# Decoder layer on one core: slots as 8-byte pairs in a prefilled list, rows gathered three tiles ahead, routing in one block with the experts

## The chip, the cores and the metric

One of the cores of a Trainium2 chip runs the whole program. TensorE (PE) multiplies, VectorE (DVE), ScalarE (ACT) and GpSimd (POOL) work element by element, SyncE (SP) issues most of the DMAs, POOL those with computed addresses. The engines run their own instruction streams and meet at semaphores. The metric is the device time in microseconds of one execution; lower is better.

## The reference

The input x is 8 sequences of 512 tokens of 256 numbers (4096 tokens), with a context of 8 x 1601 rows. Everything is float32. Three layers follow each other, each `x = layernorm(x + layer(x))`:

- a mixing layer: projections, cosine and sine phases, running sums over the sequence, gates, a layernorm and a projection;
- cross attention: 16 heads of 16 over the 1601 context rows;
- a mixture of experts: a router takes the 2 best of 8 experts for each token, softmax over the two logits gives their weights, and the result is the sum over both of `w * (relu(x @ W1[e] + b1[e]) @ W2[e] + b2[e])`, with W1 256 x 1024 and W2 1024 x 256.

## The kernel before

The program has four blocks; between two of them all engines wait for each other and for the DMAs that the block waits for.

*Mixing* (lines 220 to 1025). One sequence ("batch", b = 0 to 7) a step, the next one's projections beside this one's end. ACT writes x1 (line 769), the layer's normalized result; PE turns it for the queries (`turn`, line 492), POOL stores it to DRAM as x1_all (line 399) and prepares xbo, the residual plus bias, of the next batch (line 404); q, k and v go to DRAM as well. VectorE's products and sums are at lines 911 and 916, its wait for ACT's mean_sq ahead of line 942.

*Attention* (lines 1028 to 1353). 32 rounds, one for each batch and group of four heads. SP stores a round's result and loads the heads of the round after the next (`two_rounds`, lines 1106 to 1127; the loads at 186 to 192), then one expert's W1 a batch. For each tile of 128 context rows PE makes scores (1194), VectorE their maximum (1257), ACT the exponentials and sums (1349), POOL scales v (1321), PE multiplies (1162).

*Routing* (lines 1362 to 1716), one batch a step, two batches in the pipeline. SP loads attention's output and x1 (1442, 1444) and an expert's W2 (1450). PE projects (1516), POOL adds the output bias to x1 (1469), VectorE adds both (1594), takes mean and variance (1597, 1601), ACT the root (1564, 1566), VectorE writes x2 (1625). PE turns x2 (1529), ACT copies it (1561), PE makes the logits (1537). VectorE takes the two best (1611, 1615), their one-hot masks (1638, 1644), and with PE's ranks (1545, 1547) the slot of each token in its expert's region (1658 to 1678). Each row to be computed is written to the DRAM tensor xs as 258 numbers: the 256 of x2, the token's number and its weight. ACT makes two copies of x2 in rows_out (1575), POOL fills in the numbers (1482), waits for slot_u and issues eight indirect DMAs of 128 rows (1490); it also stores x2 as the start of the sums (1479). At the end POOL fills each region's tail with pad rows (1499, 1501), while VectorE plans the 71 tiles: the first row in xs and the expert of each (1699 to 1716).

*Experts* (lines 1719 to 1963), 71 tiles of 128 rows. SP reads a tile's row number and loads its rows (`load`, 1774 and 1775). PE turns them (1805), VectorE takes number and weight out (1904, 1905), copies the turned rows (1906) and, when the tile before has left the second halves, the expert's weights (1893 to 1895) and its scaled b2 (1898). PE multiplies by W1 (1818), ACT applies relu (1845), PE multiplies by W2 (1828), VectorE scales and adds b2 (`y_out`, 1924), and POOL adds the 128 rows to sums_all with an indirect DMA (1879), one at a time. In its order VectorE runs, in the step of tile n, `take_rows` and `weights` of tile n+1 and then y_out of tile n:

```python
                        if more:
                            v.wait_ge(mm1_done, HC // 4 * n + OPEN)
                            v.wait_ge(xs_t_ready, n + 2)
                            take_rows(after)
                            v.wait_ge(mm2_done, n + OPEN)
                            v.wait_ge(xst_copied, n + 3)
                            weights(bass.ds(n + 1, 1), after)
                        v.wait_ge(y_added[h], 16 * loads_of(it, d - 2, h))
                        v.wait_ge(mm2_done, n + 1 + OPEN)
```

Then the sums are read back, normalized (1853 to 1862) and written out, within the same block. A wait on a semaphore holds all that stands behind it on its engine.

## Time and profile before

| | us |
|---|---|
| median of 3 runs (2293.61 to 2300.70) | 2298.87 |
| the profiled execution | 2301.51 |
| its span | 2299.7 |
| busy in it: PE, DVE, ACT, POOL | 2005.8, 1765.3, 1550.1, 707.9 |

The span runs from the first to the last instruction of the profiled execution; outside it lie 1.8 us. The busy time of an engine is its instructions' alone, without waits. A tenth of the span is about 230 us; the stages have other shares than the whole, so a mean over the span says little of any of them.

### The profile page before, as it was taken

To read this page: it belongs to the slowest core of one execution; us is meant where nothing else is said; L and a number is where in the kernel's file an instruction comes from. 1 tells how busy PE (TensorE), PEld (TensorE's weight loads), DVE (VectorE), ACT (ScalarE), POOL (GpSimd) and SP (SyncE) were. 2 spreads that over 40 slices of the span, in tenths; PEclk is the share of its full clock that TensorE was granted. 3 is DMA by queue.
4 is the path that set the end of the run, shared out by engine and by line. 5 is a ranking of instruction groups with operands and counts; after the bars stand their busy time and mean duration, and the time that the engine had idled before them with its cause. 6 is when DMAs were issued, how large, how long until landed. Compare 5 with 4: busy or idle time off the path is not lost. (4 is left out here: it accounts for less than half of the span.)

```text
span 2299.7 us, 43580 instructions
## 1 busy us (share of the span) xinstructions
PE 2005.8 (87%) x10638; PEld 1059.2 (46%) x10638; DVE 1765.3 (77%) x3666; ACT 1550.1 (67%) x4346; POOL 707.9 (31%) x919
## 2 busy tenths in 40 slices
PE   6988988499999999999999998886645999999993
PEld 2454555133222232222332221113535999999993
DVE  4968875399999999999999999995653555555554
ACT  3455555399999999999999999994211333333334
POOL 0001100044444444444444441111772222333331
PEclk9989989699999999999999999997767999999997
DMA  4111103746676675775766755635732222222224
GB/s 149 42 41 69 55 23 128 148 76 104 129 130 110 131 102 124 120 122 128 112 118 115 135 105 68 97 47 177 241 123 59 37 37 37 37 37 37 37 37 156
DMA packets 130113, 217.32 MB, mean 94 GB/s; under 512 B 20290, under 2 KB 100802, under 8 KB 129938
## 3 DMA queue, kind: packets, MB, share of 16 engines
q1 hardware_dynamic: 103072, 152.25, 35.7%
q0 software_dynamic: 25440, 63.46, 10.0%
q10 hardware_dynamic: 1554, 1.05, 0.2%
q8 instruction: 20, 0.33, 0.1%
q14 instruction: 27, 0.22, 0.0%
HBM read 137.97 MB, written 78.72 MB: 94 GB/s over the span
## 5 line engine op out<-in xcount | busy, mean ns | idle before, releaser
L1349 ACT ACTIVATE probs<-psum,neg_max 128x512 f32<-128x512 f32 (+1 forms) x1664 | 1112.3, 742 | 45.9 <-DVE neg_max L1257 44.7
L1257 DVE TENSOR_REDUCE neg_max<-psum 128x1 f32<-128x512 f32 (+1 forms) x1664 | 1025.4, 676 | 18.7 <-PE psum L1194 15.3
L1194 PE MATMUL psum<-qst,kst 96*128 96x512 bf16 (+1 forms) x1664 | 530.7, 391 | 100.3 <-ACT probs L1349 61.5
L1162 PE MATMUL psum<-probs,v_scaled 128*32 128x512 f32 (+1 forms) x3328 | 450.1, 614 | 9.2 <-DVE attn L1271 9.2
L1194 PEld LDWEIGHTS psum<-qst,kst 96*128 96x128 bf16 (+1 forms) x1664 | 130.3, 98 | 688.7 <-ACT probs L1349 641.2
L1349 ACT ACTIVATION_READ_ACCUMULATOR probs<-psum,neg_max 128x1 f32 (+1 forms) x1664 | 436.1, 262 | 0.0
L1845 ACT ACTIVATE hid<-psum,b 128x128 f32<-128x128 f32 x568 | 162.5, 369 | 393.2 <-PE psum L1818 392.6
L1321 POOL TENSOR_TENSOR v_scaled<-vst,inv 128x64 f32<-128x64 f32 (+1 forms) x416 | 121.6, 292 | 687.8 <-DVE inv L1225 687.8
L1879 POOL DMA_INDIRECT sums_all<-y_out,dest x71 | 154.4, 2175 | 381.2 <-DVE y_out L1924 375.4
L1818 PE MATMUL psum<-xst,w 128*128 128x128 f32 x2272 | 266.6, 276 | 0.0
L1818 PEld LDWEIGHTS psum<-xst,w 128*128 128x128 f32 x2272 | 260.8, 193 | 0.1
L1828 PE MATMUL psum<-w,hid 128*128 128x256 f32 x1136 | 256.9, 379 | 0.0
L1828 PEld LDWEIGHTS psum<-w,hid 128*128 128x128 f32 x1136 | 210.4, 190 | 25.7
L1924 DVE SCALAR_TENSOR_TENSOR y_out<-psum,weight,b_scaled 128x256 f32<-128x256 f32 x71 | 34.3, 484 | 184.4 <-issue 177.9
L1162 PEld LDWEIGHTS psum<-probs,v_scaled 128*32 128x32 f32 (+1 forms) x3328 | 66.6, 108 | 134.1 <-issue 83.2
L1894 DVE COPY w<-w_all 128x2048 f32 x71 | 98.8, 1391 | 0.0
L1182 PE MATMUL psum<-ct,xwk 128*128 128x448 f32 x208 | 96.2, 543 | 0.0
L1177 PE MATMUL psum<-xwv,ct 128*128 128x256 f32 x364 | 93.7, 379 | 0.0
L1895 DVE COPY w<-w_all 128x2048 f32 x71 | 86.2, 1215 | 0.0
L1893 DVE COPY b<-b_cols 128x8 f32 x71 | 31.7, 447 | 60.7 <-DVE xst L1906 59.6
L1177 PEld LDWEIGHTS psum<-xwv,ct 128*128 128x128 f32 x364 | 69.2, 190 | 17.7
L1288 POOL TENSOR_SCALAR k_out<-k_f 128x448 bf16<-128x448 f32 x52 | 68.9, 1326 | 19.8 <-DVE k_f L1244 19.8
(222 smaller groups left out, 2105.8 us busy)
## 6 DMA issues: line engine op xcount, KB each, us to landing
kst<-k_parts SPq DMA_DIRECT2D x384, 112.0 KB, 6.5
k_parts<-k_out POOLq DMA_DIRECT2D x52, 336.0 KB, 3.1
w_all<-in_W SPq DMA_DIRECT2D x16, 1024.0 KB
ct<-in_ctxT SPq DMA_DIRECT2D x16, 896.0 KB, 4.7
vst<-v_all SPq DMA_DIRECT2D x64, 224.0 KB, 9.1
qst<-q_parts SPq DMA_DIRECT2D x192, 64.0 KB, 5.9
v_all<-v_out POOLq DMA_DIRECT2D x13, 896.0 KB, 4.3
rows_in<-xs SPq DMA_DIRECT2D x71, 129.0 KB, 2.0
```

The costliest lines, as they stand in the source:

```text
L1162: last = pe.matmul(psum[j * PAD:(j + 1) * PAD, 6, :], v_scaled[0:r, pb, j, :], probs[0:r, pb, j, :], start=t == 0, stop=t == ST - 1)
L1177: last = pe.matmul(psum[:, 7, (t % 2) * D:(t % 2 + 1) * D], ct1[:, k, t * P:(t + 1) * P], xwv[:, k, :], start=k == 0, stop=k == C - 1)
L1182: last = pe.matmul(psum[:, 7, 0:KC], xwk[:, part, co * P:(co + 1) * P], ct1[:, part, s0:s0 + KC], start=part == 0, stop=part == 1)
L1194: pe.matmul(psum[0:r, 2 * sbuf + i, :], kst[:, h, j, t * P:t * P + r], qst[:, h, j, :], start=True, stop=True).then_inc(scores_ready, 1)
L1257: v.tensor_reduce(neg_max[0:r, sbuf, i:i + 1], psum[0:r, 2 * sbuf + i], AX_X, ALU.min) \
L1321: pool.tensor_tensor(v_scaled[0:r, pb, :, 0:DH], vst[0:r, h, t, :].rearrange("p (j d) -> p j d", j=GH), inv[0:r, pb].rearrange("p (j o) -> ...
L1349: act.activation(probs[0:r, pb, j, :], psum[0:r, 2 * sbuf + i, :], ACT.Exp, bias=neg_max[0:r, sbuf, i:i + 1], scale=-1.0, accum_out=sums[0 ...
L1818: last = pe.matmul(psum[:, 2 + 2 * h + c // 4, (c % 4) * P:(c % 4 + 1) * P], w1[:, h, k, c * P:(c + 1) * P], xst[:, h, k, :], start=k == 0 ...
L1828: last = pe.matmul(psum[:, 6 + h, 0:D], hid[:, h, c, :], w2[:, h, c, :], start=c == 0, stop=c == HC - 1)
L1845: act.activation(hid[:, h, c], psum[:, 2 + 2 * h + c // 4, (c % 4) * P:(c % 4 + 1) * P], ACT.Relu, bias=b1[:, h, c:c + 1]).then_inc(h_read ...
L1879: pool.indirect_dma_start(sums_all, bass.IndirectOffsetOnAxis(dest[:, d, :], 0), y_out[:, h], None, compute_op=ALU.add).then_inc(y_added[h ...
L1894: v.tensor_copy(w1[:, half], w1_all[:, at].rearrange("p o c h -> p (o c) h")).then_inc(w1_ready, 1)
```

## The change

- The rows tensor xs is replaced by a list: for each slot a pair (token number, weight), 8 bytes. The list is filled beforehand, in the attention block, with pairs that name pad rows with weight 0 (`no_pairs`), so that no pads are written at the end. x2 is stored in DRAM twice, as x2_rows (which ends in 128 zero rows) and as the start of the sums, both by SP. ACT's two copies and POOL's copy of the numbers fall away; the scatters write pairs.
- A tile's rows are gathered by POOL with an indirect DMA from x2_rows. SP loads the tile's part of the list three tiles ahead into one of four places, VectorE casts the numbers (`name_rows`), POOL gathers (`gather`).
- Routing and experts are one block. The routing steps stand in straight line, three batches deep: norm of batch c, choice for c-1, ranks and slots for c-2. Projection alternates between two pairs of PSUM banks and is cut in two halves around the logits. ACT writes x2 in place of VectorE. POOL waits for nothing but slots.
- The output bias of attention is added to x1 in the mixing stage by POOL, before x1 is stored, after PE has turned it.
- w2_all is allocated from the start and lends its space to the mixing and attention stages; W2 of one expert and the routing inputs of batches 0 and 1 and xWo are loaded in the attention block, the other W2 in routing steps 3 to 7. W2 comes in an order that gives each partition 8 KB in one run.
- The semaphore wo_g_ready goes; derived_ready is waited for in its place.

The diff, cut to its core (of the removed lines only some are shown; the helpers that are not shown keep their operations):

```diff
-    ROW = D + 2
-    AT_DEST, AT_WEIGHT = D, D + 1
-    xs = nc.dram_tensor("xs", [E * REGION + P, ROW], F32, kind="Internal").ap()
+    list_all = nc.dram_tensor("list_all", [E * REGION + P, 2], F32, kind="Internal").ap()
+    x2_rows = nc.dram_tensor("x2_rows", [TOKENS + P, D], F32, kind="Internal").ap()
...
-                            wait_alone(pool, (x1_ready, e + 1))
+                            wait_alone(pool, (x1t_ready, e + 1))
+                            pool.tensor_tensor(x1, x1, rows[:, XBO:XBO + 1, :].to_broadcast([P, TT, D]), ALU.add) \
+                                .then_inc(x1bo_ready, 1)
+                            wait_alone(pool, (x1bo_ready, e + 1))
...
+                    sp.dma_start(list_all, a["no_pairs"]).then_inc(list_cleared, 16)
+                    sp.dma_start(x2_rows[TOKENS:TOKENS + P], a["no_rows"]).then_inc(list_cleared, 16)
+                    for e in range(W2_EARLY):
+                        load_w2(sp, e)
...
+                        if b == B - 2:
+                            for h in range(2):
+                                sp.wait_ge(attn_stored[h], 16 * GH * 2 * (B - 1) + OPEN)
+                                load_route(sp, h)
+                            sp.dma_start(xwo, a["xWo"].rearrange("(c p) d -> p c d", p=P)).then_inc(xwo_loaded, 16)
...
+                    def route_step(c):
+                        h = c % 2
+                        if c < B and c + 2 < B:
+                            sp.wait_ge(y2_ready, c + 1)
+                            load_route(sp, c + 2)
+                        if c < B:
+                            sp.wait_ge(x2_ready, c + 1)
+                            for rows_to in (sums_all, x2_rows):
+                                sp.dma_start(rows_to[c * L:(c + 1) * L].rearrange("(p t) d -> p t d", t=TT),
+                                             x2[:, h]).then_inc(x2_stored[h], 16)
+                        for e in W2_IN_STEP.get(c, ()):
+                            load_w2(sp, e)
...
+                    def load_list(j, d):
                         row = sp.value_load(tile_row[0:1, j], min_val=0, max_val=NO_TILE)
-                        sp.dma_start(rows_in[:, h], xs[bass.ds(row, P)]).then_inc(rows_loaded[h], 16)
-                    def tile_step(n, it, d, more):
-                        h = d % 2
-                        if more:
-                            sp.wait_ge(xst_copied, n + 1)
-                            load(bass.ds(n + 1, 1), 1 - h)
-                    load(slice(0, 1), 0)
+                        sp.dma_start(list_in[:, d], list_all[bass.ds(row, P)]).then_inc(list_loaded[d], 16)
+                    def tile_step(n, it, d, left):
+                        if left >= 3:
+                            sp.wait_ge(y_scaled, n + 1 + OPEN)
+                            load_list(bass.ds(n + 3, 1), (d + 3) % DESTS)
...
+                    sp.wait_ge(plan, ROWS_PLANNED)
+                    sp.wait_ge(scattered, 16 * 2 * TT * B)
+                    for j in range(3):
+                        load_list(slice(j, j + 1), j)
...
+                    def scatter(e):
+                        pool.wait_ge(slots_ready, e + 1)
+                        for i in range(2):
+                            for t in range(TT):
+                                at = i * TT + t
+                                pool.indirect_dma_start(
+                                    list_all, bass.IndirectOffsetOnAxis(slot_u[:, e, at:at + 1], 0),
+                                    pairs[:, e, i, t, :], None).then_inc(scattered, 16)
+                    def gather(count, d):
+                        wait_alone(pool, (dest_ready, count))
+                        pool.indirect_dma_start(rows_in[:, d % 2], None, x2_rows,
+                                                bass.IndirectOffsetOnAxis(dest[:, d, :], 0)) \
+                            .then_inc(rows_loaded[d % 2], 16)
+                    def tile_step(n, it, d, left):
+                        h = d % 2
+                        if left >= 3:
+                            wait_alone(pool, (xs_t_ready, n + 2))
+                            gather(n + 4, (d + 3) % DESTS)
+                        wait_alone(pool, (y_scaled, n + 2 + OPEN), (y_added[1 - h], 16 * loads_of(it, d - 1, 1 - h)))
+                        pool.indirect_dma_start(sums_all, bass.IndirectOffsetOnAxis(dest[:, d, :], 0), y_out[:, h], None,
+                                                compute_op=ALU.add).then_inc(y_added[h], 16)
+                    for i in range(2):
+                        pool.tensor_copy(pairs[:, :, i, :, 0], dest_ids[:].rearrange("p (b t) -> p b t", b=B)) \
+                            .then_inc(numbered, 1)
+                    pool.wait_ge(numbered, 2)
+                    pool.wait_ge(list_cleared, 32)
+                    for e in range(B):
+                        scatter(e)
+                    for h in range(2):
+                        pool.wait_ge(x2_stored[h], 16 * B)
+                    for n in range(2):
+                        gather(n + 1, n)
+                    wait_alone(pool, (xs_t_ready, 1))
+                    gather(3, 2)
...
+                    def route_step(c):
+                        if 0 <= c - 2 < B:
+                            ranks(c - 2)
+                        if 0 <= c - 1 < B:
+                            turn(c - 1)
+                        if c + 1 < B:
+                            project(c + 1, (0, 1))
+                        if 0 <= c - 1 < B:
+                            route(c - 1)
+                        if c + 1 < B:
+                            project(c + 1, (2, 3))
...
+                    def route_step(c):
+                        h = c % 2
+                        if 0 <= c - 1 < B:
+                            wait(act, logits_z_ready, c - 1)
+                            act.wait_ge(x2t_ready, c)
+                            act.activation(x2t[:], psum[:, 4:6], ACT.Copy).then_inc(x2t_copied, 1)
+                        if c < B:
+                            act.wait_ge(moments2_ready, c + 1)
+                            act.activation(rstd2_ln[:], moments2[:, :, 1], ACT.Ln, bias=eps_col[:]).then_inc(act_ln2, 1)
+                            act.wait_ge(act_ln2, c + 1)
+                            act.activation(rstd2[:], rstd2_ln[:], ACT.Exp, scale=-0.5).then_inc(rstd2_ready, 1)
+                            wait(act, x2_stored[h], 32 * (c // 2))
+                            wait(act, x2t_ready, c - 1)
+                            act.wait_ge(rstd2_ready, c + 1)
+                            act.wait_ge(shift2_ready, c + 1)
+                            for t in range(TT):
+                                last = act.activation(x2[:, h, t], y2[:, t], ACT.Identity, bias=shift2[:, t:t + 1],
+                                                      scale=rstd2[:, t:t + 1])
+                            last.then_inc(x2_ready, 1)
+                        if 0 <= c - 1 < B:
+                            act.wait_ge(gap_ready, c)
+                            act.activation(egap[:], gap[:], ACT.Exp).then_inc(egap_ready, 1)
...
+                    def route_step(c):
+                        if c < B:
+                            norm_rows(c)
+                        if 0 <= c - 2 < B:
+                            slots(c - 2)
+                        if c < B:
+                            shift_rows(c)
+                        if 0 <= c - 1 < B:
+                            choose(c - 1)
...
+                    def name_rows(d, count):
+                        v.wait_ge(list_loaded[d], count)
+                        v.tensor_copy(dest[:, d], list_in[:, d, 0:1]).then_inc(dest_ready, 1)
...
+                            v.wait_ge(y_scaled, n + 1 + OPEN)
+                            scale_bias(copy_weights(bass.ds(n + 1, 1), 1 - h), (d + 1) % DESTS)
+                        if left >= 3:
+                            v.wait_ge(y_added[1 - h], 16 * loads_of(it, d - 1, 1 - h))
+                            name_rows((d + 3) % DESTS, 16 * (it + (d + 3) // DESTS + 1))
...
+        "W2": w[f + "W2"].reshape(E, -1, P, D).transpose(0, 2, 1, 3).reshape(E, P, -1),
+        "no_rows": np.zeros((P, D), np.float32),
+        "no_pairs": np.stack([slot % P + B * L, 0 * slot], axis=1).astype(np.float32),
```

## Rows read from the trace of the kernel before

**Rows 1.** The stages: length, busy us of each engine, granted clock, DMA share, GB/s.

```profile
0.00:443.20 443.20, 355.67 (x1172) 199.27 (x1172) 286.11 (x392) 218.51 (x352) 42.63 (x62) 0.91 0.28 83
443.20:1580.60 1137.40, 1052.28 (x5564) 305.94 (x5564) 1110.83 (x2256) 1118.24 (x3328) 414.95 (x689) 0.98 0.61 106
1580.60:1749.40 168.80, 82.12 (x356) 71.31 (x357) 82.07 (x385) 30.49 (x49) 95.89 (x97) 0.65 0.57 198
1749.40:2265.20 515.80, 515.70 (x3548) 482.68 (x3546) 271.40 (x562) 163.74 (x569) 152.86 (x70) 1.00 0.22 35
2265.20:2299.70 34.50, 0.00 (x0) 0.00 (x0) 14.94 (x73) 19.08 (x48) 1.55 (x1) 0.54 0.65 247
```

**Rows 2.** The chain that ended last, its tail: start us, length us, what.

```profile
2266.43 3.66 DMA sums_all<-y_out,dest
...
2277.98 2.06 ACT w_all L1862 x4
```

**Rows 3.** Groups of the routing stage: busy us, mean ns, idle before, releaser.

```profile
L1490 POOL DMA_INDIRECT xs<-rows_out,slot_u x64 | 62.7, 980 | 38.2 <-DVE slot_u L1678 20.4 <-issue 17.8
L1516 PE MATMUL psum<-xwo,at_in 128*128 128x256 f32 x128 | 42.3, 502 | 12.6 <-DMA x_in<-x_all 11.2 <-DVE y L1594 1.4
...
L1537 PE MATMUL psum<-router_w,x2t 128*128 128x8 f32 x128 | 26.5, 345 | 29.3 <-ACT x2t L1561 29.3
```

**Rows 4.** Waits of the whole run: who for whom, us, times, longest.

```profile
DVE var_c L942 <- ACT mean_sq L744: 66.4, 8, 12.7
...
ACT rows_out L1575 <- DMA xs<-rows_out,slot_u: 38.7, 6, 8.7
```

**Rows 5.** Timeline of the routing stage's opening: start, length, engine, line, operation.

```profile
1587.62 5.78 PE L1516 MATMUL psum<-xwo,at_in 128*128 128x256 f32 x16 [11.21 <-DMA x_in<-x_all]
...
1597.34 1.38 DVE L1625 TENSOR_SCALAR x<-y,moments,rstd 128x256 f32<-128x256 f32 x4 [0.67 <-ACT rstd L1566]
...
1612.67 0.17 DVE L1678 CAST slot_u<-slot_f 128x8 uint32<-128x8 f32 x1
...
1613.78 1.06 POOL L1490 DMA_INDIRECT xs<-rows_out,slot_u  x1 [10.28 <-DVE slot_u L1678]
```

**Rows 6.** Timeline of the routing stage's end.

```profile
1720.56 0.97 POOL L1490 DMA_INDIRECT xs<-rows_out,slot_u  x1 [0.30 <-issue]
...
1742.37 0.35 SPq L1775 DMA_DIRECT2D rows_in<-xs  x1
...
1744.21 15.98 SPq L1775 DMA_DIRECT2D rows_in<-xs  x4
...
1749.45 5.09 PE L1818 MATMUL psum<-xst,w 128*128 128x128 f32 x32
```

**Rows 7.** Issue to landing of the loads of one tile's rows.

```profile
DMA to landing us min/median/max: 1.9/2.0/4.7
```

**Rows 8.** Timeline of one steady expert tile.

```profile
2004.51 0.49 DVE L1924 SCALAR_TENSOR_TENSOR y_out<-psum,weight,b_scaled 128x256 f32<-128x256 f32 x1 [2.52 <-issue]
...
2005.75 2.18 POOL L1879 DMA_INDIRECT sums_all<-y_out,dest  x1 [5.07 <-DVE y_out L1924]
...
2008.90 0.34 DVE L1898 TENSOR_SCALAR b_scaled<-b_all,weight 128x256 f32 x1
```

**Rows 9.** Issue to landing of the summing DMA, 2000 to 2100 us.

```profile
DMA to landing us min/median/max: 4.2/4.4/4.5
```

**Rows 10.** Timeline of the mixing stage: three products beside a POOL operation.

```profile
216.73 5.77 DVE L916 TENSOR_TENSOR w_all<-w_all 128x1024 f32<-128x1024 f32 x3
...
222.53 1.23 DVE L916 TENSOR_TENSOR w_all<-w_all,key_cos 128x1024 f32<-128x1024 f32 x1
```

**Rows 11.** The DMA queues: packets, MB, share of 16 engines.

```profile
q1 hardware_dynamic: 103072, 152.25, 35.7%
...
q10 hardware_dynamic: 1554, 1.05, 0.2%
```

**Rows 12.** The DMA queue's timeline early in the attention stage.

```profile
490.95 0.36 SPq L186 DMA_DIRECT2D qst<-q_parts  x1
```

More of the change, by code:

```diff
@@ L1799, in _, with project @@
                 @block.tensor
                 def _(pe):
-                    def turn(half, count):
+                    def project(b, ts):
+                        h = b % 2
+                        if ts[0] == 0:
+                            wait(pe, y2_ready, b - 1)
+                            pe.wait_ge(route_loaded[h], 32 * (b // 2 + 1))
+                        for t in ts:
+                            at = psum[:, 2 * h + t // 2, (t % 2) * D:(t % 2 + 1) * D]
+                            for k in range(C):
+                                last = pe.matmul(at, at_in[:, h, k, t * P:(t + 1) * P], xwo[:, k, :], start=k == 0,
+                                                 stop=k == C - 1)
+                        if ts[-1] == TT - 1:
+                            last.then_inc(proj_ready, 1)
@@ new lines, in turn, with route @@
+                    def turn(e):
+                        wait(pe, x2t_copied, e)
+                        pe.wait_ge(x2_ready, e + 1)
+                        for k in range(C):
+                            for t in range(TT):
+                                last = pe.transpose(psum[:, 4 + k, t * P:(t + 1) * P],
+                                                    x2[:, e % 2, t, k * P:(k + 1) * P], ident[:])
+                        last.then_inc(x2t_ready, 1)
+                    def route(e):
+                        wait(pe, logits_ready, e)
+                        pe.wait_ge(x2t_copied, e + 1)
+                        for t in range(TT):
+                            for k in range(C):
+                                last = pe.matmul(psum[:, 6, t * E:(t + 1) * E], x2t[:, k, t * P:(t + 1) * P],
+                                                 router_w[:, k, :], start=k == 0, stop=k == C - 1)
+                        last.then_inc(logits_z_ready, 1)
@@ L1832, in _ @@
                     opened(pe, mm1_done, mm2_done)
-                    turn(0, 16)
+                    pe.wait_ge(xwo_loaded, 16)
+                    project(0, range(TT))
+                    for c in range(B + 2):
+                        route_step(c)
+                    pe.wait_ge(slots_ready, B)
+                    take(0, 16)
                     tiles(pe, tile_step)
```

662 lines of the change are left out of this document (267 added, 395 removed).

## The prediction

> **What bounds the kernel now.** I read the page's first lines, then cut the span at the stage borders and asked for each engine's busy time in each stretch [rows 1]; only there is it seen that the stages have different limits. The mixing stage takes 443 us with PE the fullest engine; the attention stage takes 1137 us and ScalarE is busy for 1118 of them; the routing stage takes 168.8 us with no engine over 57% and the granted clock at 0.65, so it is bound by waits; the expert stage takes 515.8 us and PE is busy in 515.7 of them at full clock, 71 tiles at 7.26 us each; the last normalization takes 34.5. Only the routing stage has time to give without taking work off a full engine. There the waits [rows 4] name the place: ScalarE, which copies x2 into the 258-wide rows, stood 38.7 us in six waits for the scatter DMAs of two batches before, because the row buffers have two halves. And the groups [rows 3] say what a batch costs: 64 scatters of 0.98 us with about 0.3 us between two [rows 6], 1.28 us each, so 10.2 us of POOL a batch; POOL also adds a bias, stores and copies in each batch.
>
> **The routing stage, step by step.** Before, the stage opens at 1580.6, its first expert matmul starts at 1749.45 [rows 1, 6].
>
> *The opening.* The loads of the first two batches and of xWo move into the attention stage, where the queue has room (DMA share 0.61, [rows 1]) and the last round takes 35.5 us (1137.4 over 32). So the first projection starts at about 1580.8, not at 1587.62 [rows 5]: 6.8 us earlier. From there to the first slots I sum: projection 5.8; from its end (1593.40) to the start of x 3.9, by the same rows; shift 0.2 (an estimate, by the small cast of 0.17 in [rows 5]); x2 on ScalarE 2.1, by four pieces of the same size in [rows 2]. That is 1592.8. Then PE runs one whole step in its order: turn, half a projection, logits, half a projection, ranks. The copy of x2t is under the first half of the projection, choosing under the second. At the slow level that is some 12 us (below), so 1604.9. VectorE has the third batch's norm ahead of the slots (about 3.4 us, the 3.9 without ScalarE's part, from 1603.6, when that projection is done), then the slot arithmetic, some 2.2 us (an estimate: a dozen operations of the cast's size, [rows 5]): 1609. Before, it was 1612.84 [rows 5]. The three-deep order thus gives back 3 us of the 6.8.
>
> *The scatters.* POOL no longer waits on ScalarE's copy (it is gone with the rows), nor does it add, copy or store in between: 64 x 1.28 = 81.9 us from 1609.8, end at 1691.7, if slots come at least every 10.2 us. The pads (8 scatters and one store) go. Do the slots come that fast? PE was busy 82.1 us in the stage, 10.3 us a batch: 5.3 projection, 3.3 logits, 1.7 transposes and ranks [rows 1, 3]. In the new order PE is a nearly closed loop (logits, choosing, ranks, turn), so I take 10.3 plus 0.4 for semaphores: 10.7 us a batch. Seven of those from 1609, then 0.8 and 10.2: last scatter generated at 1694.9. Bounds: 1691.7 if PE gets warmer, since POOL is then the limit; 5.8 for the projection at its slowest [rows 5], 3.3 and twice 1.7 for the rest make 12.5 and 1707.5, if PE is slow throughout.
>
> *Under cover:* x2's two stores and the W2 loads are on SP's queue. From the fourth step this is about 3 MB in 10.7 us, 280 GB/s, where the stage now moves 198 and the last stage reaches 247 [rows 1]. So a route load behind a W2 load can come late by a few us; I price it at 0 to 10 us and take it into the range, not the sum.
>
> *The pairs as packets.* A scatter has 128 of them, 8 for each of 16 engines. SP's queue took 35.7% of 16 spans for 103,072 packets of 1.5 KB on average, 127 ns each [rows 11]; 8 are 1.0 us, under POOL's 1.28, so the sum stays 43. The Trainium skill ("DMA: Bandwidth & Descriptors", "Specifications") says that below 512 B the engine reads, modifies and writes, which speaks against this part; no row here shows its price. If it doubled a packet's time, the scatters would end 48 us later and the gain would be lost (last rival).
>
> *From the last scatter to the first expert matmul.* Landing 2.2 us after generation (4.4 less 2.18, [rows 8, 9]); reading the row number and issuing the first list load 1.4 (1742.37 to 1744.21 less one other issue, [rows 6]); landing 2.0 [rows 7]; cast 0.2; POOL's gather starts 0.75 after its release, as the summing DMA does after y_out (2005.00 to 2005.75, [rows 8]), and takes 0.98; the second 1.3 later; landing 2.2; transposes 0.7. Sum 11.6, so the first expert matmul is at 1706.5. Before, from the last scatter's end at 1721.53 it took 27.9 us, with the pads, a wait for them and a block border. **Saved: 1749.45 - 1706.5 = 43 us.** Bounds 46 and 30.
>
> **The expert stage.** PE issues the same matmuls and has no gap, so nothing is gained. New is a ring. Counted from the start of y_out of tile n-1 (2004.51 in [rows 8]): the summing DMA starts at 1.24 and lands 4.4 later [rows 9], at 5.64; only then may VectorE, free since 4.7, cast the list's numbers of tile n+3 into that slot, 0.2; POOL starts the gather 0.75 later and takes G; then it prepares the next summing DMA, 0.3 (between two scatters, [rows 6]) to 0.75. Queued behind that cast on VectorE is y_out of tile n, and PE waits for it two tiles on. The ring takes 5.65 + G to 6.1 + G. No gather is in the trace. The near end is the plain scatter, G = 0.98, the far end the summing DMA, 2.18. At 0.98 the ring takes 6.6 to 7.1, under the tile's 7.26: cost 0, which I take, since a gather is also a plain copy of one row a partition. At 2.18 it takes 7.8 to 8.3, so 40 to 72 us over 70 tiles; in the middle, 1.58, 0 to 30. The list load is issued about 1.5 us after y_out and lands by 4: hidden. The casts that leave the place between turn and weights (0.15 us) are not waited for by PE.
>
> **The mixing stage.** POOL's bias add comes after PE's turn, ahead of x1's store and the next xbo; the store is then some 4 us later, and the next x1 a whole step away. It holds VectorE: three products of 1.23 each took 5.77 beside the xbo add [rows 10], 2.1 too many. So 2.1 more a batch on VectorE. But VectorE waits 66.4 us in eight places for ScalarE's mean_sq [rows 4], 8.3 each, behind these products. Cost 0; if all of it showed, 8 x 2.1 = 17 us.
>
> **The attention stage.** ScalarE's work is untouched; other buffers, same shapes: 0. New on SP's queue are three DMAs at its opening (list, zero rows, one W2) and five loads near its end; the first is a rival's place (below).
>
> **The sum.** The profiled execution took 2301.5 us with a span of 2299.7. Less 43: 2258.5. It lies 2.6 above the median of the runs, 2298.9; I forecast 2258 for the new kernel's median, and hold 2246 to 2272 for this case.
>
> **The rivals.**
> *The ring in the expert stage is the bound.* The DMA's completion, a cast and two POOL issues in series leave only 0.2 to 0.6 us. For it: G is unknown. Against it: VectorE is idle when the gather would run, and the weight copies that run beside the summing DMA are over. At G of 1.6 and a little above, 10 to 30 us: 2268 to 2288; at the far end 2298 to 2330. Decides when G plus preparation is over 1.6 us. 0.14.
> *Routing is fed late.* PE stays at the lower of its two levels (1.2 GHz), or route loads wait behind W2. For it: clock 0.65 in the stage. Against: PE is denser. Costs 7 to 13: 2265 to 2271, and up to 10 more with the queue. 0.14.
> *The list's fill stalls attention: slower.* SP issues the fill (33,920 pairs of 8 bytes, DRAM to DRAM) at about 444, and head loads stand behind it in the same queue. If it goes out pair by pair, each of 16 engines has 2120 packets. The nearest prices: 1554 packets in 0.2% of 16 spans, 47 ns each; on SP's queue 35.7% for 103,072, 127 ns [rows 11]. That is 100 or 269 us. The next heads are issued at 490.95 [rows 12], needed at 514 (two rounds of 35.5 after 443), so it may take some 70 us; above that attention stops: 30 or 199 us, so 2288 to 2457. Decides for the sign at 53 ns a packet (70 us and the 43 saved). Against: both sides are contiguous, and as long runs 0.27 MB take 1 to 2 us at the 247 GB/s of [rows 1]. 0.06. The Trainium skill ("DMA: Bandwidth & Descriptors", "Why a DMA increments its semaphore by 16 and not by 1") says one descriptor moves one contiguous run of the last dimension, here 8 bytes, which speaks for this rival; it also says that software can split a contiguous row.
> *It does not do what it says: small writes are no cheaper.* At twice 127 ns a scatter keeps the engines 2.0 us, 64 take 130 us instead of 82: 2306. For it: packets so small are nowhere in the trace by themselves. Against: the 47 ns above. 0.04.
>
> **How the numbers follow.** Forecast 0.62, ring 0.14, fed late 0.14, fill 0.06, small writes 0.04. A measurement here tells about 0.3% (7 us) from no change. The first three are faster, but for the ring's far end (0.01): 0.89. The low ends of the fill, the small writes and the ring's far end are near 2299: 0.03 for the same, 0.08 slower. Range 2243 to 2286: below, 5 us for slots that come earlier at a warm clock and a shorter tail; above, nearly all of the ring and of the late feeding; fill and small writes stay outside.
>
> **What would show it.** One block from 1580.6 on; 64 scatters with no gap over 1 us, first near 1610, last near 1695; first expert matmul near 1707; then transposes every 7.25 us, POOL with a gather of about 1 us some 6.9 us into each tile. Wrong: a tile of 7.4 us or more (ring); gaps between batches of scatters (fed late); PE idle in the first 200 us of attention (fill); DVE waits for mean_sq under 3 us a batch with a longer mixing stage.

## The result and the profile after

The changed kernel takes 2266.1 us (median of 4 runs, 2265.05 to 2271.26), the kernel before 2298.7 beside it (2293.6 to 2300.7): ratio 0.987, 95% interval 0.985 to 0.989, so 33 us faster. Forecast were 2258 and a range of 2243 to 2286. The profiled execution took 2271.3 us with a span of 2269.6, 30.1 less than before. The stages of the profile after, as in [rows 1] (length, busy us of each engine, granted clock, DMA share, GB/s):

```profile
0.00:434.67 434.67, 353.49 (x1164) 197.58 (x1172) 302.91 (x392) 218.47 (x352) 61.55 (x70) 0.91 0.29 84
434.67:1571.90 1137.23, 1052.32 (x5564) 305.66 (x5564) 1110.87 (x2256) 1117.51 (x3328) 415.17 (x689) 0.98 0.62 109
1571.90:1718.10 146.20, 70.71 (x356) 61.58 (x357) 61.61 (x350) 31.27 (x65) 65.94 (x69) 0.71 0.61 167
1718.10:2235.00 516.90, 516.88 (x3548) 483.82 (x3546) 264.42 (x488) 161.90 (x568) 183.45 (x139) 0.99 0.22 36
2235.00:2269.60 34.60, 0.00 (x0) 0.00 (x0) 14.94 (x73) 19.08 (x48) 1.56 (x1) 0.56 0.65 246
```

The 30.1 us are 22.6 from routing (168.8 to 146.2), 8.5 from mixing (443.2 to 434.7), 0.2 from attention, less 1.1 in the expert stage and 0.1 in the tail. The forecast had 43 from routing and nothing from the others. So the total is near by two errors of opposite sign: the mechanism that was forecast gave half of its 43 us in this run, and luck gave 8.5 back. Both are followed up below.

Groups of routing after, against [rows 3] (busy, mean ns, idle before and its releasers):

```profile
L1568 POOL DMA_INDIRECT list_all<-pairs,slot_u x64 | 63.3, 989 | 71.8 <-DVE slot_u L1812 53.8 <-issue 18.0
L1617 PE MATMUL psum<-area 128*128 128x256 f32 x128 | 35.5, 431 | 5.3 <-PEq L1141 4.7 <-DMA area<-x_all 0.6
...
L1637 PE MATMUL psum<-router_w,w 128*128 128x8 f32 x128 | 20.0, 292 | 13.9 <-issue 7.0 <-ACT w L1709 6.9
```

The scatter costs what was forecast (0.98 plus 0.3), TensorE's work shrank from 82.1 to 70.7 us as the clock rose, but GpSimd still waits 53.8 us for slots. The waits say what stands behind that (who for whom, us, times, longest):

```profile
POOL list_all L1568 <- DVE slot_u L1812: 53.8, 6, 24.6
ACT egap L1725 <- DVE gap L1838: 38.2, 4, 13.4
DVE logits L1828 <- remote: 36.5, 3, 14.0
...
ACT w L1709 <- remote: 15.9, 2, 8.0
```

"remote" means that the increment of the semaphore which ended the wait was recorded at that moment, but that no instruction which makes it ended near it. The timeline of the first of the five such waits:

```profile
1602.52 1.92 PE L1637 MATMUL psum<-router_w,w 128*128 128x8 f32 x16
...
1604.08 0.25 DVE L1817 SCALAR_TENSOR_TENSOR shift<-moments,rstd 128x4 f32<-128x4 f32 x1
...
1604.29 1.97 PE L1617 MATMUL psum<-area 128*128 128x256 f32 x8
...
1607.43 0.64 SPq L185 DMA_DIRECT2D w_all<-in_W  x1
...
1616.11 0.97 POOL L1568 DMA_INDIRECT list_all<-pairs,slot_u  x1 [0.30 <-issue]
1618.32 0.19 DVE L1828 TENSOR_TENSOR logits<-psum,router_b 128x32 f32<-128x32 f32 x1 [13.99 <-remote]
```

VectorE's next instruction waits only for TensorE's logits of the third batch, and by the profile their matmuls are over by 1604.44; TensorE had even gone on to the next projection. Still VectorE stands until 1618.32, with TensorE and ScalarE behind it. The others are at the fifth and eighth batch's logits (9.90 and 12.62 us) and at ScalarE's fifth and seventh copy of x2t (8.00 and 7.86): 52.4 us in all, of which GpSimd's backlog hides about half.

All five wait for TensorE, and the trace also records when a semaphore was raised. For these logits that is 1618.29, which is 13.9 us after the end of the matmul that raises it and 0.03 before VectorE goes on. The other four signals are recorded 5.6 to 8.0 us after their matmuls, and each time the waiting engine goes on within 0.08 us. So VectorE and ScalarE are not slow to see a signal that is there: TensorE's signal comes late. (The ends of matmuls are modelled in the profile, so it can't be told whether the signal alone is late, or the result with it.)

From the last scatter to the first expert matmul (against [rows 6, 7]):

```profile
1706.44 0.97 POOL L1568 DMA_INDIRECT list_all<-pairs,slot_u  x1 [0.30 <-issue]
1710.64 4.30 SPq L1531 DMA_DIRECT2D list_in<-list_all  x4
1712.47 0.15 DVE L1912 CAST dest<-list_in 128x1 uint32<-128x1 f32 x1 [7.72 <-DMA list_in<-list_all]
1713.46 1.00 POOL L1575 DMA_INDIRECT rows_in<-x_rows,dest  x1 [6.06 <-DVE dest L1912]
...
1718.13 1.27 PE L1679 MATMUL psum<-xst,w 128*128 128x128 f32 x5
```

10.7 us from 1707.41 on; forecast 11.6. Next, one turn of the ring in the expert stage (against [rows 8]):

```profile
2004.62 1.64 POOL L1586 DMA_INDIRECT sums_all<-y_out,dest  x1 [0.60 <-issue]
...
2008.61 0.15 DVE L1912 CAST dest<-list_in 128x1 uint32<-128x1 f32 x1 [1.04 <-DMA sums_all<-y_out,dest]
2009.53 0.98 POOL L1575 DMA_INDIRECT rows_in<-x_rows,dest  x1 [3.26 <-DVE dest L1912]
...
2010.62 0.48 DVE L1935 SCALAR_TENSOR_TENSOR y_out<-psum,list_in,b_scaled 128x256 f32<-128x256 f32 x1 [1.85 <-PE psum L1689]
...
2011.87 1.71 POOL L1586 DMA_INDIRECT sums_all<-y_out,dest  x1 [1.36 <-issue]
```

The gather takes 0.98 us and ends 5.9 us after the summing DMA began; GpSimd could issue the next one 0.3 to 0.6 later, and does so at 7.25, when y_out lets it. So the ring fits with about 0.8 to 1.0 us to spare.

### The profile page after: what moved, and what is told of

It reads as the page before. It is cut to its first block and busy times, and to the rows that moved or that the text cites. A ratio compares the mean times of both kernels' runs of the same rounds, so it can differ in the third digit from the quotient of the medians.

```text
span 2269.6 us, 43525 instructions
## 1 busy us (share of the span) xinstructions
PE 1993.4 (88%) x10630; PEld 1048.6 (46%) x10638; DVE 1754.7 (77%) x3559; ACT 1548.2 (68%) x4361; POOL 727.7 (32%) x967
## 5 line engine op out<-in xcount | busy, mean ns | idle before, releaser
L1400 ACT ACTIVATE w_all<-psum,neg_max 128x512 f32<-128x512 f32 (+1 forms) x1664 | 1111.4, 737 | 46.3 <-DVE neg_max L1308 44.4
L1308 DVE TENSOR_REDUCE neg_max<-psum 128x1 f32<-128x512 f32 (+1 forms) x1664 | 1025.3, 676 | 18.5 <-PE psum L1245 14.9
L1213 PE MATMUL psum<-w_all 128*32 128x512 f32 (+1 forms) x3328 | 450.5, 615 | 9.8 <-DVE w_all L1322 9.8
L1400 ACT ACTIVATION_READ_ACCUMULATOR w_all<-psum,neg_max 128x1 f32 (+1 forms) x1664 | 428.3, 257 | 0.0
L1372 POOL TENSOR_TENSOR w_all<-vst,inv 128x64 f32<-128x64 f32 (+1 forms) x416 | 121.0, 291 | 687.5 <-DVE inv L1276 686.7
L1689 PE MATMUL psum<-area,hid 128*128 128x256 f32 x1136 | 256.9, 379 | 0.0
L1689 PEld LDWEIGHTS psum<-area,hid 128*128 128x128 f32 x1136 | 210.4, 190 | 25.7
L462 PE MATMUL psum<-w_all 128*128 128x512 f32 x384 | 192.7, 653 | 25.1 <-DMA w_all<-in_xWq 16.7
L953 DVE TENSOR_TENSOR w_all<-w_all 128x1024 f32<-128x1024 f32 (+1 forms) x88 | 131.4, 1530 | 1.5
L1233 PE MATMUL psum<-area,xwk 128*128 128x448 f32 x208 | 96.2, 543 | 0.0
L1228 PE MATMUL psum<-xwv,area 128*128 128x256 f32 x364 | 93.6, 379 | 0.0
```

The costliest lines, as they stand in the source:

```text
L462: last = pe.matmul(psum[:, bank + co, :], weights[:, k, co * P:(co + 1) * P], rhs(k), start=k == 0, stop=k == chunks - 1)
L953: v.tensor_tensor(out_t, in0, in1, op).then_inc(dve_front, 1)
L1213: last = pe.matmul(psum[j * PAD:(j + 1) * PAD, 6, :], v_scaled[0:r, pb, j, :], probs_at[pb][0:r, j, :], start=t == 0, stop=t == ST - 1)
L1233: last = pe.matmul(psum[:, 7, 0:KC], xwk[:, part, co * P:(co + 1) * P], ct1[:, part, s0:s0 + KC], start=part == 0, stop=part == 1)
L1308: v.tensor_reduce(neg_max[0:r, sbuf, i:i + 1], psum[0:r, 2 * sbuf + i], AX_X, ALU.min) \
L1372: pool.tensor_tensor(v_scaled[0:r, pb, :, 0:DH], vst[0:r, h, t, :].rearrange("p (j d) -> p j d", j=GH), inv[0:r, pb].rearrange("p (j o) -> ...
```

## The experiments

Twelve kernels ran. The first four ask what holds VectorE and ScalarE up, and where the mixing stage's 8.5 us are from. "Opening" below is ScalarE's table load, the first thing in the routing block. "Idle times" are the waits over 5 us that the profile puts down to "remote".

For what follows it matters where they ran. Experiments 1 to 4 were timed on one chip, 5 to 8 on a second and 9 to 12 on a third, each time beside the kernel before, whose medians were 2296.7, 2293.5 and 2295.7 us. The changed kernel itself ran on neither of the last two, so 5 to 12 have no changed kernel beside them. On which chip the first pair ran is not on record.

**1. W2 hardly loaded.**

```
 def load_w2(sp, e):
+    if e >= W2_EARLY:
+        sp.dma_start(w2_all[:, e, 0, 0:16], a["W2"][e][:, 0:16]).then_inc(ffn_loaded, 16)
+        return
...
-    v.tensor_copy(w2[:, half], w2_all[:, at]...)
+    v.tensor_copy(w2[:, half], w2_all[:, 0:1]...)
```

> The changed kernel, but the seven W2 loads of the routing stage carry 64 bytes a partition instead of 8192, and every expert takes expert 0's W2 (the output is then that of other weights; the work per tile is the same). Theory A: the long idle times of one engine in the changed kernel's routing (VectorE 14.0, 9.9 and 12.6 us, ScalarE 8.0 and 7.9 us, each with everything it waits for done) are loads of its own instructions that stand behind the bulk transfers which SP issued just before. Then without the 7 MB no such idle time is over 4 us, the stretch from routing's opening to the first expert matmul falls from 146.4 us to 120 to 130, and the kernel's time from 2266 to about 2245. Rival R: routing is now written out for eight batches and each engine runs through its instructions faster than they arrive, whatever else is moved. Then the idle times stay at 8 to 14 us, the stretch at 146 and the time at 2266.

Measured: 2264.0 us, opening to first expert matmul 138.6 us. VectorE's idle times are 15.57 and 13.27 us, ScalarE's one 6.91; the first is again before the third batch's logits. Theory A is refuted: 7 of 24.5 MB less in the stage left three idle times of five and took nothing off the first, and the kernel gained 2 us where 21 were expected.

**2. W2 in short rows.** As the kernel before loads it; the input is laid out accordingly.

```
-    sp.dma_start(w2_all[:, e], a["W2"][e].rearrange("p (c d) -> p c d", c=HC))...
+    sp.dma_start(w2_all[:, e], a["W2"][e].rearrange("(c p) d -> p c d", p=P))...
```

> The changed kernel, but W2 is loaded as the kernel before loads it, in rows of 1024 bytes (1024 rows an expert) instead of 8192 (128 rows an expert), at the same places in the program. Theory A2: what holds the instruction loads up is the length of W2's rows. Then the long idle times fall under 4 us, routing takes 125 to 135 us instead of 146.4 and the kernel about 2250. Theory A1: what holds them up is the amount that is in flight. Then routing stays at 143 to 150 us and the time at 2263 to 2270. Rival R (the instructions themselves) expects no change either.

Measured: 2272.7 us (2264.3 to 2276.2), routing 143.1. VectorE 13.67, 9.70 and 11.03 us, ScalarE 7.62 and 5.73. The length of the rows is not it. (The Trainium skill, "DMA: Bandwidth & Descriptors", section on queues, rings and completion order, says that an engine changes between queues only after a whole packet of several descriptors; by that, long rows should hold up other queues more. The idle times of this run show no such difference.) The mixing stage of this execution ended at 443.3.

**3. No bias in the mixing stage.**

```
-    wait_alone(pool, (x1t_ready, e + 1))
-    pool.tensor_tensor(x1, x1, rows[:, XBO:XBO + 1, :]..., ALU.add).then_inc(x1bo_ready, 1)
-    wait_alone(pool, (x1bo_ready, e + 1))
+    wait_alone(pool, (x1_ready, e + 1))
```

> The changed kernel, but GpSimd's bias add in the mixing stage is left out, and the wait before it goes back to that of the kernel before (the bias is then missing from the output). Asked is why the mixing stage ends at 434.7 us instead of 443.2, which was not predicted. Theory M1: it comes from the new place of GpSimd's store, after the transposes. Then the stage ends near 443 again and the time is about 2274. Theory M2: it comes from something else (other places in SBUF, or how the clock is granted in one execution). Then the stage ends at 433 to 436, the time is 2262 to 2266, and VectorE's wait for mean_sq goes back from 41 to about 66 us, as nothing of GpSimd's lies beside its products.

Measured: 2266.5 us, mixing ends at 437.2. That is against M1 and 1 us beyond M2's range; as one and the same mixing code ends anywhere from 434.7 to 445.4 in these profiles (table below), one execution does not settle it. VectorE's wait for mean_sq is 59.1 us against 41.4 with the bias add: the add costs VectorE 2.2 us a batch, as forecast (2.1), and no time of the kernel that these runs can tell. Idle times in routing: 14.9, 11.74 (VectorE), 6.88, 6.26 (ScalarE).

**4. The kernel before with W2 in long rows.** The edit of 2, backwards.

> The kernel before, but with W2 in rows of 8192 bytes as the changed kernel has it. Theory A2 (long rows hold up the instruction loads): idle times of 8 to 14 us appear in its routing too, which takes 180 us or more instead of 168.8, and the time is 2310 or more. Theory A1 (the amount in flight) and rival R: routing stays within 3 us of 168.8 and the time within 3 us of 2299, perhaps a little less, since fewer rows are moved.

Measured: 2294.9 us against 2296.7, ratio 0.999 (0.9975 to 1.0005); routing 168.4. No effect, as A1 and R had it.

Left was the stream of scatters, which in the changed kernel runs without a gap, and VectorE's instructions themselves. The releases at 1618.3, 1648.8 and 1690.8 all come 1.2 to 2.5 us after GpSimd's last scatter of a row.

The traces at hand say more on both. The page lists the DMA queues that carry instructions:

```profile
q8 instruction: 22, 0.36, 0.1%
q14 instruction: 29, 0.24, 0.0%
```

In the changed kernel and in experiments 1 to 3 there are 17 idle times. In 14 of them no packet of these two queues moved at all, and in the other three the last one had landed 7.3 us or more before the idle time ended. That is against a late load of instructions, in theory A as in rival R. And TensorE's signals are late in the kernel before too, by up to 3.7 us (experiment 4: 3.7). In both kernels of the first pair ten of them are over 0.4 us late, and seven of the ten come 1.2 to 2.7 us after GpSimd's last scatter of a row; none is late before the first scatter. The kernel before scatters in rows of 10 us, the changed one opens with a row of 20. This fits theory S below, as far as these six profiles go.

**5. All scatters at the end.**

```
-    pool.wait_ge(slots_ready, e + 1)
+    pool.wait_ge(slots_ready, B)
```

> The changed kernel, but GpSimd issues none of the 64 scatters until the slots of all eight batches are there. Theory S: the long idle times of VectorE and ScalarE in routing (13.99, 9.90, 12.62, 8.00, 7.86 us) are TensorE's increments of semaphores arriving late while GpSimd issues scatters back to back; they ended 1.2 to 2.5 us after the end of such a stream, or in a gap of it. Then VectorE and ScalarE have no idle time over 5 us before the last slots, the steps keep the 8.2 us of the first ones, the last slots are there some 82 us after routing's opening (in the changed kernel 124), and the 64 scatters take 82 us behind them: first expert matmul 82 + 82 + 11 = 175 us after opening, time near 2295. Rival R: the idle times belong to the instructions (written out for eight batches, they must be loaded). Then they stand at the same instructions with the same lengths, the last slots come at 124 us and the time is near 2335.

Measured: 2301.6 us (one run; about 2295 was expected). In the waits of this kernel's routing no "remote" is left:

```profile
ACT w L1709 <- PE psum L1627: 17.6, 8, 3.5
DVE logits L1828 <- PE psum L1637: 12.3, 8, 4.8
```

Slots of the last batch 81.6 us after opening (82 expected), 64 scatters in 82.7, first expert matmul 176.0 after opening (175). Theory S forecast this, and rival R did not: VectorE's program runs through when GpSimd is silent. But this is the second chip, and no kernel on it shows an idle time, whether GpSimd is silent (5) or not (8), so the run can't be set against the changed kernel's of the first pair. What it does price is the small writes: 64 scatters in a row go out every 1.29 us, and TensorE starts 11 us behind the last, so they don't hold the queue up.

**6 and 7. Pauses in the stream.** In 6 each batch waits for the eight scatters before it, in 7 (two semaphores in turn, for which `numbered` gives way) each scatter for the one two before.

```
 def scatter(e):
     pool.wait_ge(slots_ready, e + 1)
+    wait(pool, scattered, 16 * 2 * TT * e)          # 6
...
+    wait(pool, scattered[n % 2], 16 * (n // 2))     # 7, ahead of each
```

> The changed kernel, but each batch of eight scatters waits until the eight before have landed, which puts a pause of some 2.2 us behind each. Theory S: the pauses let the increments through, the long idle times end at the latest with the batch (under 7 us each), and the last scatter ends sooner or at most as late as in the changed kernel (135.5 us after opening): 24 + 8 x 12.5 = 124 us; time 2255 to 2262. Rival R: idle times of 14, 8 and 10 us as before, at the same instructions, and the pauses come on top where GpSimd is late: time 2266 to 2275.

> The changed kernel, but at most two scatters are in flight: each waits until the one two before it has landed (two semaphores in turn). Theory S1: what delays the increments is scatters that pile up. Then no idle time over 5 us is left; a scatter takes 1.3 to 1.6 us, the last ends 24 + 64 x 1.5 = 120 us after opening or sooner, time 2250 to 2262. Theory S2: it is GpSimd's issuing itself, however few are in flight. Then the idle times stay near 14, 10 and 8 us unless the wait opens gaps between scatters. Rival R: they stay, at the same instructions.

Measured: 6 takes 2286.3 us (ratio to the kernel before 0.996, 0.994 to 0.998), 7 takes 2315.9 (1.009, 1.006 to 1.012); both forecasts, 2250 to 2275, are missed. No "remote" in either, but the waits cost more than the idle times did. GpSimd in 6, first scatter of each of the later batches:

```profile
1617.63 0.97 POOL L1569 DMA_INDIRECT list_all<-pairs,slot_u  x1 [9.81 <-DMA list_all<-pairs,slot_u]
1635.54 0.97 POOL L1569 DMA_INDIRECT list_all<-pairs,slot_u  x1 [8.02 <-DMA list_all<-pairs,slot_u]
...
1712.95 0.96 POOL L1569 DMA_INDIRECT list_all<-pairs,slot_u  x1 [2.86 <-DMA list_all<-pairs,slot_u]
```

GpSimd stands 2.9 and 3.1 us for the last two landings, when little else moves, and 5.7 to 9.8 us for the four earlier ones, beside the stores and W2; my 2.2 is below all of them. In 6 VectorE waited for no late signal, although each row of eight scatters was as dense as in the kernel before, where such rows go with signals up to 3.7 us late. So either the scatters alone do not make a signal late, or they do so on one chip and not on another; these runs don't separate the two.

**8. Forty more instructions on VectorE.**

```
+    for n in range(40):
+        v.memset(pairs[:, n // 8, n % 2, n % 8 // 2, 1:2], 0.0)
     v.tensor_copy(slot_at[:, 0], region_at[:]).then_inc(plan, 1)
```

> The changed kernel with 40 more small VectorE instructions (fills of 4 bytes a partition) ahead of routing's first step, where VectorE has idle time. Rival R, loading of instructions at fixed places of VectorE's program: the first long idle time moves by 40 instructions, about one step earlier, from before the third batch's logits to before the second's or another instruction. Theory S: it stays before the third batch's logits with 13 to 16 us. In both the time is within 3 us of one of the changed kernel's (2265 to 2276).

Measured: 2250.3 us (one run), 16 less than the changed kernel on its chip, and below what either theory had. The fills took 1.13 us in VectorE's idle time. Its stages from routing on:

```profile
1572.40:1697.40 125.00, 68.93 (x357) 59.07 (x358) 62.24 (x390) 31.61 (x65) 66.67 (x69) 0.73 0.74 196
1697.40:2214.00 516.60, 516.60 (x3547) 483.83 (x3546) 264.31 (x488) 162.44 (x568) 184.53 (x139) 0.99 0.23 36
```

and the same moment as above in its timeline:

```profile
1602.84 1.71 PE L1637 MATMUL psum<-router_w,w 128*128 128x8 f32 x14
...
1604.18 0.35 DVE L1817 SCALAR_TENSOR_TENSOR shift<-moments,rstd 128x4 f32<-128x4 f32 x1
...
1604.59 0.19 DVE L1828 TENSOR_TENSOR logits<-psum,router_b 128x32 f32<-128x32 f32 x1
```

The stream began at 1597.07 (1596.88 in the changed kernel) and ran as densely, and every signal of TensorE's is recorded within 0.06 us of its matmul's end, here and in the whole trace. VectorE's waits for logits (28.2 us in all, the longest 9.4) now end with the matmuls that make them. Routing takes 125.0 us, 43.8 less than before. What TensorE waits for now are late loads of rows:

```profile
PE psum L1617 <- DMA area<-x_all: 14.5, 4, 7.1
```

**9 to 12. Is it the place in a block of instructions? Does it hold? And W2 spread.** The number of fills in 8 set to 256 or 128 (into y2's place); 8 again; and 8 with W2's loads one a step:

```
-    W2_IN_STEP = {3: (1,), 4: (2,), 5: (3,), 6: (4, 5), 7: (6, 7)}
+    W2_IN_STEP = {e: (e + 1,) for e in range(7)}
```

> The changed kernel with 256 more small VectorE instructions ahead of routing's first step (at 28 ns each, as 40 of them took 1.13 us, 7.2 us, of which 4.8 lie in VectorE's first wait). With 40 more, all five long idle times were gone, so their cause depends on where VectorE's instructions lie. Theory P256: what counts is the place within a block of 256 instructions (the size that the Trainium skill gives). Then 256 more puts every instruction back at its old place, and the idle times of 14, 8, 10 us return, the first before the third batch's logits: time 2266 to 2276. Rival Q: it is no matter of such a place; any shift against the changed kernel, or chance, takes them away. Then none over 10 us: time 2250 to 2262 by whether the mixing stage takes 435 or 443 us.

> The same with 128 more instructions (3.6 us, within VectorE's first wait). Theory P256: half a block off, no long idle time before the third batch's logits, time 2250 to 2262. Theory P128 (blocks of 128): as the changed kernel, 14 us before the third batch's logits and 2265 to 2272. Rival Q: no long idle times, 2250 to 2262.

> The kernel with 40 more small VectorE instructions once more, timed in five rounds. If the 2250.3 us of its one run belong to the program, the median is 2248 to 2260 (the upper end where the mixing stage takes 443 us), its interval lies below the changed kernel's 2266, and routing takes 125 us to the first expert matmul with the 64 scatters in one row of 89 us. If that run was chance, the median is near 2266 and the idle times of 14, 8 and 10 us are in the trace.

> The kernel with 40 more instructions, and W2's loads spread: one in each of the routing steps 0 to 6, instead of one in steps 3 to 5 and two in steps 6 and 7. With 40 more instructions TensorE waited 2.7, 4.3 and 7.1 us for loads of rows in routing. If GpSimd's 64 scatters set routing's length (89 us in one row after the first slots, theory G), the spread gains nothing: time within 3 us of the kernel with 40 more. If the late row loads count (theory L), up to 7 us are gained. If bulk transfers in the first steps delay the first slots (theory M), 1 to 5 us are lost.

Measured: 256 more, 2249.8 us; 128 more, 2246.2 (one run each); 40 more again, 2253.0 (2249.6 to 2259.1), ratio to before 0.9817 (0.980 to 0.983); spread, 2259.2, ratio 0.9845 (0.983 to 0.986). In none of the four is an idle time of the old kind. What P256 and P128 forecast did not come (the block of 256 instructions is the Trainium skill's, "Advanced Engine Details and Errata", "ISA Cache"). But they forecast it as a return to the changed kernel's state, and the changed kernel was not seen on this chip, so neither is tested. Rival Q had the times right, but so would a rival that was not written down: that the idle times belong to the chip, or to what it was doing, and that no edit is needed to be rid of them. Of the kernels that ran on this chip the one with 40 more beats the kernel before by 1.8%; 128 more may be as good or better, which one run can't tell. Spreading W2 loses 6 us against it in the same comparison: routing 133.3 instead of 124.4, slots later (GpSimd waits 39.7 us for them, against 30.6), TensorE's wait for rows 16.0 instead of 13.0. That is theory M's sign, and a little over its 1 to 5 us; the times of the two kernels overlap (2256.3 to 2261.9 with the spread).

The profiled executions side by side (us; routing is opening to first expert matmul; "latest" is by how much the latest of TensorE's signals came after its matmul's recorded end):

```
kernel                   chip     mixing ends  routing  latest  idle times of the old kind
before                   unknown     443.2     168.8     3.7   none over 4
changed                  unknown     434.7     146.2    13.9   14.0  8.0  9.9  7.9  12.6
W2 hardly loaded (1)     first       435.4     138.6    15.3   15.6  6.9  13.3
W2 short rows (2)        first       443.3     143.1    13.8   13.7  7.6  9.7  5.7  11.0
no bias in mixing (3)    first       437.2     140.8    14.7   14.9  6.9  6.3  11.7
before, W2 long rows (4) first       441.9     168.4     3.7   none over 3
scatters last (5)        second      436.9     176.0     0.1   none
batch landed (6)         second      436.5     160.7     0.1   none
two in flight (7)        second      445.4     181.4     0.1   none
40 more (8)              second      435.8     125.0     0.1   none
256 more (9)             third       435.6     126.3     0.1   none
40 more again (10)       third       440.8     124.4     0.1   none
W2 spread (11)           third       434.9     133.3     0.1   none
128 more (12)            third       434.8     124.5     0.1   none
```

The line falls between the chips and not between the edits. The six profiles above it have late signals whatever the kernel, and each lacks the record of 4 to 8 of TensorE's 2653 signals; the eight below have none late, and every record. What would decide is the changed kernel on the second or third chip, or the kernel with 40 more on the first.

## Why the prediction was right, and where it was not

**Routing's scatters: the mechanism right, the size right only once the idle times are gone.** 64 scatters at 1.29 us set the stage, as forecast, and the saving of 43 us is what the kernel with 40 more instructions shows on the second chip (43.8), its last scatter ending 113.5 us after the opening (forecast 114.3). The changed kernel itself saved 22.6. The step that failed is a batch of slots every 10.7 us: GpSimd waited 29.2 us for them after the first (53.8 less 24.6; 6.0 with 40 more), since VectorE or ScalarE stood 8 to 14 us for signals of TensorE's that came 5.6 to 13.9 us late. I had looked for such a cost in a cold TensorE or late row loads (the rival "fed late", 7 to 13 us); neither was it. TensorE's clock rose to 0.71, and the row loads cost 0.6 us on TensorE where the idle times hid them, 14.5 where they are gone, mostly hidden behind GpSimd's backlog.

**Why the signals are late is not settled.** Shown: the idle times come in all four kernels in which routing's programs on VectorE and GpSimd are those of the change, the first always before the third batch's logits, at 13.7 to 15.6 us. All 17 end with a signal of TensorE's that is recorded 3.6 to 15.3 us after its matmul. It is not W2's amount or the length of its rows. It is hardly a load of instructions, as none landed in the 7 us before any of the idle times ended. Late signals go with GpSimd's rows of scatters in the first six profiles, in the kernel before as well. Not shown: whether anything in experiments 5 to 12 took them away. Those ran on other chips, and there no signal was late in any kernel. The place within 128 or 256 instructions is untested for the same reason.

**Opening.** Forecast were 28.4 us from opening to the first slots, measured 24.0: I had taken the slow clock for a whole step, and a step takes 8.2 us (slot casts at 1595.78 and 1604.00), not 12.

**Tail of routing.** 11.6 forecast (its terms add up to 11.7), 10.7 measured (11.4 with 40 more).

**Expert stage.** Cost 0 forecast, 1.1 measured between two executions; whether it is the ring's was not tried. G is 0.98, the near end, which I took. The ring takes 6.2 to 6.5 us, not 6.6 to 7.1, as the summing DMA now takes 1.64 us instead of 2.18 and lands in 3.9 instead of 4.4; why it is shorter was not tried.

**Mixing.** Forecast no change, and the part of it on the bias add holds: the bias add takes 2.2 us a batch out of VectorE's slack (experiment 3). The 8.5 us by which the stage ended earlier can't be put down to the change. Kernels with the same mixing code ended it between 434.7 and 445.4, and one and the same program at 435.8 and 440.8. The two executions of the old code lie at 441.9 and 443.2; whether a part of the difference is real is open. Left alone, the routing gain less the expert stage's 1 us makes 21 to 22 us of the 30.1, so that the total came as near to its forecast as it did is in part luck.

**The rivals.** The list's fill did not stall attention: its 265 KB moved as 16 packets of 16,960 bytes and landed 4.8 us after issue, and attention took 1137.2 us as before. Small writes are no dearer than their issue (experiment 5). The ring is not the bound. "Fed late" had the right sign, gaps between the batches of scatters, but neither of its two causes.

## What to carry to other kernels

When a stage is forecast from the cadence of its fullest engine, look in the new trace for engines that stand although all they wait for is done, and ask first whose signal it was and when it was recorded: here that turned "VectorE and ScalarE stand" into "TensorE's signals come late". An edit that makes a symptom go away has shown something only if the unchanged kernel, run beside it on the same chip, still has the symptom. The kernels with 40, 128 and 256 empty instructions look some 13 to 20 us better than the changed one (2253.0, 2246.2 and 2249.8 against 2266.1), and how much of that is the chip can't be told. A wait for a DMA's landing costs what else is in flight at that moment (2.9 us quiet, up to 9.8 beside bulk), so a limit on transfers in flight can cost more than what it cures. And compare stages, not totals: of the 20 us that this change missed in one stage, 8.5 were given back by another whose length changes from run to run.

## What the runs showed of the hardware

- An indirect scatter of 128 pairs of 8 bytes costs GpSimd 0.97 us and 0.30 before the next, one of 128 rows of 258 numbers 0.98, and a gather of 128 rows of 1 KB 0.98.
- A 4-byte fill on VectorE costs 28 ns (40 in 1.13 us).
- W2 in rows of 8192 or 1024 bytes: 2294.9 against 2296.7 us in the kernel before, no difference.
- In six profiles TensorE's increments of semaphores are recorded up to 15.3 us after the end of the matmul that makes them (3.7 in the kernel before), in the stage in which GpSimd issues scatters back to back; in the eight profiles of kernels with the changed routing on two other chips, never more than 0.06 us. Waiting engines go on within 0.08 us of the record.
